# Neighbourhood attention and mixture of experts on one core: image 0 ahead of the weights, value writes on SP's queue, scores in threes between value strips

## What is computed

```python
x = x + attention(_gn(x)); x = x + experts(_gn(x))         # _gn: 32 groups, mean and variance per image
qkv = x @ qkv_w.T + qkv_b                                   # 12 heads of 32
k_cat = concat(k, reg_k); v_cat = concat(v, reg_v)          # 16 register rows seen by all positions
scores = where(mask_cat, q @ k_cat.T / sqrt(32), -1e30)     # mask: 7 x 7 neighbourhood, clipped at the edges
o = softmax(scores) @ v_cat; attention = o @ out_w.T + out_b
# experts: softmax router over 4 experts, top 2, gelu(x @ fc1.T + b1) weighted, @ fc2.T + b2
```

## Time and profile before

| | us |
|---|---|
| median of 3 runs | 715.81 |
| lowest, highest | 713.94, 717.45 |
| profiled execution, its own time | 715.22 |
| its span, first to last instruction | 713.3 |
| TensorE matmul busy | 593.1 (83%) |
| VectorE busy | 474.6 (67%) |
| ScalarE, GpSimd busy | 296.3, 300.5 (42% each) |
| mean granted TensorE clock | 0.962 of full |

### The profile page before, as it was taken

The page is one execution under the profiler, slowest core; times in us unless marked ns, Lnnn a source line. Parts: engine busy times, 40 slices in busy tenths (PEclk is TensorE's granted clock), DMA queues, the critical chain, the costliest instruction groups (busy, mean ns, idle before and its releaser), DMA issues.

```text
span 713.3 us, 22313 instructions
## 1 busy us (share of the span) xinstructions
PE 593.1 (83%) x9225; PEld 413.9 (58%) x9225; DVE 474.6 (67%) x1024; ACT 296.3 (42%) x586; POOL 300.5 (42%) x437
## 2 busy tenths in 40 slices
PE   0686899988997887987898878988777786799997
PEld 0433777667764765566765767557555443455554
DVE  3784566777976699774866768866797476652332
ACT  2343355315632377313552246323584226533231
POOL 4312789235221745318872532216454025621331
PEclk9997999999999999999999989999899898899999
DMA  8959751895359641694429772596520000001102
GB/s 322 277 152 219 203 131 46 215 252 149 92 126 238 187 114 45 164 263 135 123 72 256 209 174 59 123 240 177 152 57 2 1 33 34 34 34 67 66 36 99
DMA packets 130940, 95.93 MB, mean 134 GB/s; under 512 B 67340, under 2 KB 125384, under 8 KB 130072
## 3 DMA queue, kind: packets, MB, share of 16 engines
q1 hardware_dynamic: 121960, 78.72, 42.5%
q0 software_dynamic: 8880, 15.79, 7.4%
HBM read 58.11 MB, written 35.54 MB: 131 GB/s over the span
## 4 chain that ended last, share of the span: by engine, by line
PE 42%; DVE 20%; DMA 15%; ACT 7%; issue 7%; POOL 5%; SPq 3%; ACTq 0%; DVEq 0%; POOLq 0%
PE ps L904 25%; PE ps L1045 6%; DMA qscr<-QT 5%; DMA vscr<-VT 4%; DVE MX L523 4%; PE ps L1026 4%; PE ps L1002 4%; POOL vscr L339 3%; DMA KB<-kscr 2%; DVE GT_ L466 2%; DMA X<-in_x 2%; DVE ST L434 2%; DVE X L517 1%; ACT KB L734 1%; DVE KT L501 1%
## 5 line engine op out<-in xcount | busy, mean ns | idle before, releaser
L523 DVE TENSOR_REDUCE MX<-ps 128x2 f32<-128x456 f32 x216 | 124.4, 626 | 63.3 <-PE ps L1002 62.3
L904 PE MATMUL ps<-XH,WQ 128*128 128x384 f16 x810 | 151.6, 344 | 13.9 <-DVE XH L473 6.4
L904 PEld LDWEIGHTS ps<-XH,WQ 128*128 128x128 f16 x810 | 80.9, 102 | 76.7 <-issue 21.4
L787 ACT ACTIVATE PT<-ps 128x448 f32<-128x448 f32 (+1 forms) x162 | 79.0, 510 | 58.8 <-PE ps L1026 57.7
L1002 PE MATMUL ps<-KB,QS 120*32 120x228 f16 x1728 | 66.1, 276 | 31.9 <-DVE MX L523 9.9
L1026 PE MATMUL ps<-QS,KB 122*128 122x112 f16 (+1 forms) x864 | 65.6, 215 | 17.2 <-ACT VT L770 7.0
L339 POOL DMA_DIRECT2D vscr<-VT x108 | 57.2, 537 | 50.3 <-ACT VT L770 45.9
L409 POOL TENSOR_TENSOR OS<-QS,OS 128x384 f16<-128x384 f32 x36 | 32.3, 912 | 101.6 <-ACT OS L879 101.6
L904 PE MATMUL ps<-OS,WO 128*128 128x384 f16 x324 | 62.4, 343 | 13.3 <-DVE X L517 12.0
L332 POOL DMA_DIRECT2D qscr<-QT x36 | 26.3, 732 | 108.8 <-DVE QT L507 108.8
L1026 PEld LDWEIGHTS ps<-QS,KB 122*128 122x128 f16 x864 | 44.3, 100 | 38.4 <-ACT PT L787 13.0
(11 more groups left out here) (159 smaller groups left out, 978.7 us busy)
## 6 DMA issues: line engine op xcount, KB each, us to landing
KB<-kscr SPq DMA_DIRECT2D x108, 192.0 KB, 7.0
kscr<-KT SPq DMA_DIRECT2D x72, 192.0 KB, 2.5
VR<-vscr SPq DMA_DIRECT2D x216, 56.0 KB
QS<-qscr SPq DMA_DIRECT2D x108, 96.0 KB, 5.6
X<-in_x SPq DMA_DIRECT2D x6, 1152.0 KB, 18.9
qscr<-QT POOLq DMA_DIRECT2D x36, 192.0 KB, 5.1
vscr<-VT POOLq DMA_DIRECT2D x108, 64.0 KB, 2.3
out<-X SPq DMA_DIRECT2D x12, 576.0 KB, 3.3
```

The costliest lines, as they stand in the source:

```text
L523: V.tensor_reduce(out=MX[:, s % 2, t, 2 * pair:2 * pair + 2], in_=ps[:, S_BANK(s, i), 0:2 * RUN].rearrange("p (h n) -> p h n", h=2), op=AL ...
L787: A(PTS[n % 4][:, 0:w], ps[:, ST_BANK(n), 0:w], ACT.Exp, scale=SCORE).then_inc(s_["exd"], 1)
L904: last = mm(bank, lhsT(a, k), rhs(b, k), start=(k == 0 and n == 0), stop=(finish and k == steps - 1 and n == 2))
```

## The change

1. The opening: image 0 is loaded first, in six halves, then the weights of group 0, then the tables, then the other weights. Image 1 is loaded half by half in stage 0's attention. In stage 0 VectorE makes all low halves, and ScalarE the float32 value of channel block 2, from which its low half is made. TensorE runs 26 extra matmuls of 232 columns before the first statistics. Group means leave out the products with blocks that share no group. `value_bias` moves behind three value strips, and `obx` with it.
2. The writes of the values to `vscr` move from GpSimd's queue to SP's, behind `queries_in` and before `values_in`.
3. In stages 1 to 5 scores come in threes, each followed by one value strip (before: six, then two). In stage 0 three value strips come first. Banks and waits follow; the last value strip has a bank of its own. The turned maxima move: on TensorE behind the fourth and the sixth three, on ScalarE behind values 2 and 4 (stage 0: behind all six).
4. In stages 2 and 5 the group parameters are made after the fourth query strip, not after the last.

```diff
@@ sync: the opening
+            for c in range(KC):
+                for half in range(2):
+                    image_in(0, c, half)
             sp.dma_start(raw_g[0], wqkv[:, 0, :]).then_inc(w_in[0], 16)
-            for c in range(KC):
-                sp.dma_start(xs(0, c, 0, N), x[0, :, c, :]).then_inc(x_in[0][c], 16)
+            sp.dma_start(QS[96:120, :, :], qtab.unsqueeze(1).broadcast_to([24, HEADS, N])).then_inc(s_["t_in"], 16)
+            for i in range(4):
+                sp.dma_start(KB[96:TROWS, :, i, :], ktab[1].unsqueeze(1).broadcast_to([26, HEADS, SLOTW])).then_inc(s_["t_in"], 16)
             for g in (1, 2):
                 sp.dma_start(raw_g[g], wqkv[:, g, :]).then_inc(w_in[g], 16)
...
-            for c in range(KC):
-                sp.dma_start(xs(1, c, 0, N), x[1, :, c, :]).then_inc(x_in[1][c], 16)
@@ sync: new function, and its place
+            def values_out(gi, s):
+                sp.wait_ge(s_["v_sb"], 6 * gi + s + 1)
+                if 36 * gi > 0:
+                    sp.wait_ge(s_["pv"], 36 * gi)
+                for b in range(KC):
+                    sp.dma_start(vscr[16 * b:16 * b + 16, CT_ * s + 3:CT_ * s + 3 + CT_, :], VT[:, s % 2, b, :]).then_inc(v_out[s % 2], 16)
...
                 for s in (4, 5):
                     queries_in(gi, s)
+                for s in range(TILES):
+                    values_out(gi, s)
                 for s in (0, 1):
                     values_in(gi, s)
...
                     values_in(gi, s + 2)
+                    if gi == 0:
+                        image_in(1, s // 2, s % 2)
@@ gpsimd
-                for s in range(TILES):
-                    values_out(gi, s)
-                    if s == 1:
-                        register_values(gi)
-                    if s in (1, 3):
-                        maxima_in(gi, s // 2)
+                register_values(gi)
+                for s in (0, 1):
+                    maxima_in(gi, s)
@@ scalar
                 for s in range(TILES):
                     values_out(gi, s)
-                    if s in (1, 3):
-                        maxima_out(gi, s // 2)
+                    if gi and s in (2, 4):
+                        maxima_out(gi, s // 2 - 1)
+                if gi == 0:
+                    for s in (0, 1):
+                        maxima_out(gi, s)
@@ tensor
+            pe.wait_ge(s_["pads"], 3)
+            for i in range(WARM):
+                mm(ps[0:LEAD, 6, 0:HEADS * LEAD], KB[0:96, 0, 0, 0:LEAD], KB[0:96, :, 0, 0:LEAD], start=True, stop=True)
...
-                for s in range(TILES):
-                    if s % 2 == 0:
-                        if s:
-                            maxima_turned(gi, s // 2 - 1)
-                        for i in range(6):
-                            scores(gi, s // 2, i)
-                    for b in range(KC):
-                        values(gi, s, b)
+                if gi == 0:
+                    for s in range(3):
+                        all_values(s)
+                    value_bias()
+                for k in range(6):
+                    three_scores(k)
+                    if gi:
+                        all_values(k)
+                    elif k < 3:
+                        all_values(3 + k)
```

More of the change, by code:

```diff
@@ L36 @@
 GN_STEPS = KC * STRIPS
-POOL_K = ((0,), (0, 2), (0, 2), (0, 2))
+WARM = 26
+POOL_K = ((), (0, 2), (0, 2), (0, 2))
 def query_rows(a):
@@ L184, in build @@
         K_BANK = (4, 6, 2, 3, 5, 7)
-        V_BANK = (2, 3, 2, 3, 2, 3)
+        V_BANK = lambda gi, s: 1 if gi and s == TILES - 1 else 2 + s % 2
         Q_BANK = lambda s: 2 + s % 2
@@ L287, in _ @@
                     values_in(gi, s + 2)
+                    if gi == 0:
+                        image_in(1, s // 2, s % 2)
+                if gi == 0:
+                    for half in range(2):
+                        image_in(1, 2, half)
             sp.wait_ge(s_["st_mm"], 36 * STAGES)
@@ L566, in _ @@
                     if gi == 0:
-                        for k in range(KC):
+                        for k in range(2):
                             normalised(0, a, k)
                         for k in range(KC):
-                            if k not in POOL_K[0]:
-                                low_half(0, a, k)
+                            low_half(0, a, k)
                         if a == 0:
@@ L590, in _ @@
                         V.tensor_tensor(BVH[:, 1, :], cols["bv"], BVH[:, 0, :], ALU.subtract).then_inc(s_["bvlo"], 1)
-                    if gi == 0 and s == 5:
-                        dve.wait_ge(s_["bv_mm"], 1)
-                        V.scalar_tensor_tensor(out=cols["obx"], in0=ps[:, 1, 0:KC], scalar=1 / WS, in1=cols["ob"],
-                                               op0=ALU.mult, op1=ALU.add).then_inc(s_["obx"], 1)
                     if gi and s:
                         projected(gi - 1, s - 1)
+                    if gi in (2, 5) and s == 3:
+                        parameters(gi // KC + 1, 0)
                 if gi:
                     projected(gi - 1, TILES - 1)
-                if gi in (2, 5):
-                    parameters(gi // KC + 1, 0)
                 for s in range(3):
@@ L603, in _ @@
                         maximum(gi, s, i)
+                        if gi == 0 and s == 0 and i == 2:
+                            dve.wait_ge(s_["bv_mm"], 1)
+                            V.scalar_tensor_tensor(out=cols["obx"], in0=ps[:, 7, 0:KC], scalar=1 / WS, in1=cols["ob"],
+                                                   op0=ALU.mult, op1=ALU.add).then_inc(s_["obx"], 1)
                     split_maxima(gi, s)
@@ L624, in _ @@
                             if gi == 1 and s == 0 and a < 3:
-                                dve.wait_ge(x_in[1][a], 16)
+                                for half in range(2):
+                                    dve.wait_ge(x_in[1][a][half], 16)
                             last = block_statistics(1 if gi == 1 else 0, a % 3, j)
@@ L910, in group_means @@
                 for j in range(KC):
-                    for k in range(KC):
-                        last = mm(ps[:, bank, 2 * j:2 * j + 2], G[:, k, j * P:(j + 1) * P], mv[:, k, :], start=(k == 0), stop=(k == KC - 1))
+                    near = [k for k in range(KC) if abs(k - j) < 2]
+                    for k in near:
+                        last = mm(ps[:, bank, 2 * j:2 * j + 2], G[:, k, j * P:(j + 1) * P], mv[:, k, :], start=(k == near[0]), stop=(k == near[-1]))
                 last.then_inc(s_["gn_mm"], 1)
@@ L983, in scores @@
                     pe.wait_ge(qs_in[s], 48 * (gi + 1))
-                if i == 5 and s in (1, 2) or i == 1 and s >= 3:
+                if i == 0 and s == 2:
+                    pe.wait_ge(s_["t_ev"], 6 * gi + 1)
+                if i == 0 and s == 3:
+                    pe.wait_ge(s_["v_sb"], 6 * gi + 6)
+                if i == 1 and s >= 3:
                     pe.wait_ge(s_["t_ev"], 6 * gi + s)
+                if gi == 0 and s == 0 and i == 5:
+                    pe.wait_ge(s_["obx"], 1)
                 if s == 0:
@@ L1074, in _ @@
                     pe.wait_ge(s_["kr_lo"], 1)
-                    pe.wait_ge(s_["obx"], 1)
                 if gi in (1, 2):
```

86 lines of the change are left out of this document (47 added, 39 removed).

## The result

The changed kernel takes 763.69 us (median of 4 runs, 760.43 to 765.09); the kernel before took 715.27 in the runs beside it (713.94 to 717.45). The ratio is 1.069, with a 95% interval of 1.064 to 1.074: slower by 48 us. The forecast was 756, with a range of 718 to 774. The profiled execution took 763.04 us by its own time, with a span of 761.2.

The account below looks back on a forecast made before the run. No engine bounds the kernel throughout; a stage's middle part is nearly full of transfers, so their order matters. 715.2 + 33.7 (writes) + 7 (key load) + 3.6 (clock) - 4.5 (opening) + 1 (image 1) = 756 us, range 718 to 774.

Parts of the forecast that it names:

- Q: Time in each stage when SP's nine query loads end; forecast as the earliest a moved value write can leave.
- The write term, +33.7: Middle part of each stage: value writes in SP's queue delay the first weighted matmul, 33.7 us in sum over six stages.
- W: Time of the first weighted() matmul on VR in each stage, where attention starts in earnest; forecast at Q + 17.1 us.
- Fifth key load, +7: Stages 1 to 5, behind the value reads: the load lands late, a new TensorE wait of 1.4 us each, +7 us.
- clock, +3.6: TensorE drops to its slow clock level after the new waits: 0.9 us in each of four stages, +3.6 us (0 to 9).
- image 1's +1: Stage 0's attention: image 1's later load, 576 KB ahead of the sixth key load, costs +1 us.
- The opening, -4.5: Start of the kernel: image 0 ahead of weights, halves and fewer group products save 4.5 us (6.5 to 3).
- Costed at nothing: Middle part: scores in threes, early group parameters in stages 2 and 5, and GpSimd's freed issuing, all priced at zero.
- Order costs little: Rival, chance 0.16: SP's writes as cheap as its loads, quick landings, key load on time, clock holds; 731 us.
- Losses and the opening cancel: Rival, chance 0.09: strip 5's queries come some 5 us earlier a stage without GpSimd's traffic beside them; 715 us.
- Behind the loads: Rival, chance 0.12: each stage's first write waits in SP's queue for loads' data, landing in 5.2 not 2.4 us; 773.
- Faster: Rival, chance 0.11: TensorE waited for the value loop through GpSimd's queue; 18 us go and the opening counts fully; 693 us.

Follow-up runs that it names:

- e1: The changed kernel with the 18 value writes of a stage back on GpSimd's queue: 718.97 us, ratio 1.006.
- e2: The kernel before with only the value writes moved to SP's queue, behind the queries: 770.27 us, ratio 1.079.
- e8: The changed kernel with three value buffers instead of two (SUMT as the third): 755.79 us, ratio 1.057.
- e6: The changed kernel with strip 0's value reads placed behind the write of strip 3 instead of strip 5: 765.95 us, ratio 1.070.
- e12: The changed kernel with the value reads of strips 0 and 1 issued by GpSimd, writes still on SP: 745.28 us, ratio 1.044.
- e5: The changed kernel with SP's order altered, value writes placed before and between the query loads of strips 4 and 5: 756.57 us, ratio 1.056.
- e10: The changed kernel with the value writes issued by ScalarE, each strip's three behind its copy: 739.8 us, ratio 1.039.
- e3: The kernel before with only the new opening, image 1 loaded later in stage 0's attention: 716.62 us, ratio 1.004.
- e9: The kernel before with the new opening, but image 1 loaded in the opening behind the weights: 718.52 us, ratio 1.007.
- e4: The kernel before with only scores in threes, the new middle-part order and early group parameters, writes on GpSimd: 717.82 us, ratio 1.004.
- e11: The kernel before with a third value buffer (SUMT), writes on GpSimd as they were: 708.47 us, ratio 0.992.

## Why the prediction was right or wrong

- **Direction and mechanism: right.** e1 and e2 show it from both sides: taking the writes out of SP's queue removes the loss but for some 4 us, putting them there alone makes 55 us. What I said would be seen is there: 18 writes in one row from Q on, the third copy waiting for a transfer, a wait before weighted() of 4.57 us, and Q unmoved against the stage's start.
- **The write term, +33.7, was too small: W - Q grew by 44.6.** I had W at Q + 17.1 and it came at Q + 19.0. The step that failed is the price of a write on SP. I took 0.53 from GpSimd's rows, with 0.647 as the upper bound. The row of writes lasts 13.6 to 15.6 us where I had 12.6, and without its waits for copies 12.8 on average: 0.71 a write. e8, which has nearly no waits in it, needs 0.75. The landing was sized about right: the third copy comes 4.5 us after the first write on average (76.80 - 72.38 = 4.4 in stage 0), of which 2.3 are issues, which leaves 2.2 against my 2.4. The waits for copies were smaller than mine, 1.6 us a stage against 2.9, since the landings passed beside issues that took longer.
- **My picture of the loop was too simple.** I added one chain. The runs show two floors under W: the third value copy + 10 us of TensorE's work, and the start of strip 0's reads + 4 us. In the changed kernel the reads decide. Lift them (e6, e12) and the copy decides a few us below, so each single remedy gave back a part only: nothing (e6, for the waits behind W), 7 us (e5), 8 (e8), 18 (e12), 24 (e10). With the rest of the change in place, only e1, the writes on GpSimd, has neither the reads behind all writes nor the dearer issues.
- **Fifth key load, +7, and clock, +3.6: the sum was near, the split wrong.** Together with image 1's +1 I had 11.6 and measured 9.0 from W on. But 6.9 of the 7.0 us in stages 1 to 4 are TensorE's longer busy time at a lower granted clock: that term is the larger one, since the slow level lasts beyond the four matmuls that I counted. Behind W the waits for key loads grew too, but less than I had: in stages 0 to 4 they are 7.4 us in sum, against 3.7 before. In stage 1 it is 0.59 us and not 1.4, by the timeline of TensorE of the changed kernel:

```profile
190.69 0.57 PE L1027 MATMUL ps<-KB,QS 120*32 120x228 f16 x16 [0.59 <-DMA KB<-kscr]
```

- **The opening, -4.5: the size was near, its worth wrong.** Q of stage 0 came 6.7 us earlier. The timeline of TensorE of the changed kernel has the group means and the first keys:

```profile
18.74 3.12 PE L928 MATMUL ps<-SM,G 128*128 128x2 f32 x14 [4.71 <-DVE SM L444]
26.37 5.40 PE L919 MATMUL ps<-XH,WQ 128*128 128x384 f16 x18 [3.21 <-DVE XH L480]
```

Against the earlier trace rows the group means begin 2.1 us earlier and not 3.6, and take 0.85 less, as said. The weights came later than I took, but stayed hidden. The rest I hadn't counted: VectorE's strips follow every 3.33 us and no longer every 3.85, with GpSimd out of them (read from the traces, not tried by itself). Yet e3, e1 and e9 show that nothing of it is left at the end, and that part stays unexplained.
- **Costed at nothing: threes and parameters.** e4 shows +2.5 us with the writes on GpSimd. Whether the cover that I named, the wait for the writes, hides them in the changed kernel no run shows: with the writes on SP the threes and the opening together are worth -7 (763.7 against 770.3), and Q of stage 0 alone comes 6.7 us earlier.
- **The rivals.** "Order costs little" (731) fell with the price of a write. "Losses and the opening cancel" needed an earlier Q within the stage; from the stage's start it is 188.4 us in sum against 188.5. "Behind the loads" asked for a first landing of 5.2 and the rows give 2.2 (3.4 at most), so its 773 was near the result for another reason. In e5, where query loads stand around the first writes, that landing is 4.4 on average in stages 1 to 5 (3.4 to 6.6, from the end of the strip's last issue to the third copy). From GpSimd in e1, stage 1, it is no shorter: issued by 154.24, third copy at 160.37, 6.1. These rows speak for the traffic of the moment as what sets the landing, and not for who issues. "Faster" named the value loop as what TensorE waited for; this change can't show it, but e11 does, for some 6 us and not for 18.

At one more place a page bears on this. The Trainium skill (DMA: Bandwidth & Descriptors, Issuing engines are not separate DMA queues) says that issuing from several engines saves only the time that a sequencer needs to start a transfer, "usually small relative to the DMA itself". The first half agrees with the landings above. The second half does not hold here: a write lands in 2.1 us and its issue takes 0.6 to 0.75, and 18 issues in a row, ahead of the reads, are the larger part of these 44.6 us: in e8, with nearly no landing left in the row, W - Q is still 6.2 of the 7.4 us a stage above the kernel before.

## What to carry to other kernels

A transfer's price is not only its landing but its place in a queue that issues one thing at a time: count the issues between the last thing that must precede a read and the read itself, and price them at a run of the same kind on the same queue. Look for the second floor before trusting a remedy: moving one milestone (W in e6 came up to 4.6 us earlier) is worth nothing when the next wait stands a few us behind it. A buffer more in the loop that the trace shows waiting was worth 0.8% here, while reordering a full queue was worth little.

## What was not expected of the hardware

The durations of SP's value writes in the changed kernel, from the view of their line (shortest, median, longest in ns), and their landing:

```profile
L257 SPq DMA_DIRECT2D vscr<-VT x108: 517/598/1651, 72.4 to 539.9; - x108
...
DMA to landing us min/median/max: 1.9/2.1/3.9
```

The same writes took GpSimd 528 ns at the median and 611 at most; on SP the median is 598, the longest 1651, and in a nearly unbroken row (e8) the pace was 0.75 us a write, not 0.6: single writes take up to three times the shortest. What holds those up no run here shows. From ScalarE's queue (e10) the median was 622 ns. They land as fast from SP as from GpSimd: 2.1 against 2.3 at the median.

The move changed more than the queue's order. By the pages of e1 and of the changed kernel the same 7.08 MB left the queue q0 (software_dynamic) for q1 (hardware_dynamic), and with them 3456 packets became 15552: 455 bytes each and no longer 2048. Whether this makes an issue dearer on SP no run here tests.

Behind the waits of 3.7 to 4.8 us before weighted() TensorE ran at the slow level for 4 to 6 us (in stage 1 until 184.7, 3.9 us after W, by the granted clock), and its busy time in stages 1 to 4 grew by 1.5 to 2.1 us each.
